# Attention and mixture of experts on one core: expert 0's rows transposed on TensorE, its list made tile by tile, and three steps moved

## The reference

```python
x = x + xattn(layernorm(x), ctx)      # 16 heads of 32; 2048 keys; q, k, v and the
                                      # probabilities rounded to 8-bit steps
n = layernorm(x)
w = golden_weights(n, Wr, temperature)   # a weight per token and expert, most are 0
x = x + sum_e w[:, e] * ((silu(n @ Wg[e]) * (n @ Wu[e])) @ Wd[e])   # 8 experts, F = 512
```

## Time and profile before

| | before |
|---|---|
| median of 3 runs | 807.9 us (807.88, 807.9, 809.99) |
| the profiled execution, its own time | 809.75 us |
| its span in the trace | 807.8 us |
| TensorE busy | 626.9 us (78%) |
| VectorE busy | 585.9 us (73%) |
| ScalarE busy | 449.8 us (56%) |
| GpSimd busy | 378.2 us (47%) |
| mean granted TensorE clock | 0.907 |

### The profile page before, as it was taken

How to read it: one execution, slowest core, us unless ns; L and a number is a source line. 1 busy time by engine, 2 the same in 40 slices (tenths; PEclk the granted TensorE clock), 3 DMA queues, 4 the chain that set the end, 5 groups by cost and what they waited for, 6 DMA issues and landing times.

```text
span 807.8 us, 15841 instructions
## 1 busy us (share of the span) xinstructions
PE 626.9 (78%) x4937; PEld 293.1 (36%) x4937; DVE 585.9 (73%) x1096; ACT 449.8 (56%) x519; POOL 378.2 (47%) x422
## 2 busy tenths in 40 slices
PE   2999898665867676777777654039999999999993
PEld 0444333132434242434333333014444444444441
DVE  4897687998999999999999954707446365374430
ACT  4243347587888888888888882004343443353321
POOL 2354343634566676767575751113353344334403
PEclk9999989698999998988999976559999999999997
DMA  8967749699998989898989895365987966967714
GB/s 246 263 139 163 167 79 165 120 175 210 173 167 167 186 168 183 163 188 156 196 155 201 153 191 134 97 195 83 232 217 164 243 170 172 254 140 204 140 15 54
DMA packets 339468, 134.97 MB, mean 167 GB/s; under 512 B 313700, under 2 KB 313700, under 8 KB 339432
## 3 DMA queue, kind: packets, MB, share of 16 engines
q1 hardware_dynamic: 332264, 117.76, 67.9%
q0 software_dynamic: 7168, 16.78, 10.2%
HBM read 44.33 MB, written 12.58 MB: 70 GB/s over the span
## 4 chain that ended last, share of the span: by engine, by line
PE 38%; issue 15%; SPq 14%; DMA 12%; DVE 9%; POOL 8%; ACT 2%; POOLq 1%; DVEq 0%; ACTq 0%
PE psum L1286 35%; DMA work<-work 8%; SPq L402 7%; SPq L313 2%; DVE spare L1082 2%; POOL work L563 2%; ACT work L820 1%; SPq L387 1%; POOL work L586 1%; PE psum L1393 1%; PE psum L1450 1%; DMA work<-x_rows,slot_tok 1%; DVE work L916 1%; DMA token_region<-work 1%; DMA work<-in_L_xattn_Wq_dram 1%
## 5 line engine op out<-in xcount | busy, mean ns | idle before, releaser
L820 ACT ACTIVATE work<-spare,exp_bias 128x2048 uint8<-128x2048 f32 (+1 forms) x128 | 256.2, 2002 | 54.3 <-DVE exp_bias L1089 47.2
L1082 DVE TENSOR_SCALAR_CACHE_REDUCE spare<-psum,q_step_now,s_first 128x1024 f32<-128x1024 f32 x128 | 171.0, 1338 | 1.5 <-PE psum L1393 1.3
L1082 DVE TENSOR_SCALAR_CACHE_REDUCE spare<-psum,q_step_now 128x1024 f32<-128x1024 f32 x128 | 164.4, 1286 | 5.9 <-PE psum L1393 5.8
L563 POOL CAST work<-work 128x2048 int16<-128x2048 uint8 x64 | 120.9, 1894 | 91.7 <-DMA work<-work 78.3
L1393 PE MATMUL psum<-keys_region,work 128*128 128x512 f16 x256 | 91.3, 456 | 42.8 <-DVE spare L1082 39.8
L667 POOL DMA_INDIRECT work<-x_rows,slot_tok x32 | 51.8, 1618 | 120.6 <-DVE slot_w L1226 81.2
L1359 PE MATMUL psum<-values_region,work 128*128 128x32 f16 x2048 | 73.0, 179 | 37.6 <-DMA work<-work 35.0
L1393 PE MATMUL psum<-keys_region,bias_hl 128*128 128x512 f16 x256 | 80.8, 413 | 27.3 <-DVE spare L1082 27.3
L1286 PE MATMUL psum<-work,spare 128*128 128x512 f16 x384 | 86.2, 385 | 18.4 <-DMA work<-work 18.4
L1359 PEld LDWEIGHTS psum<-values_region,work 128*128 128x128 f16 x2048 | 69.0, 98 | 84.3 <-DMA work<-work 54.0
L679 POOL DMA_INDIRECT out_dram<-keys_region,slot_tok x32 | 50.4, 1576 | 85.6 <-ACT keys_region L882 78.0
(11 more groups left out here) (188 smaller groups left out, 905.4 us busy)
## 6 DMA issues: line engine op xcount, KB each, us to landing
spare<-in_L_ffn_Wg_dram SPq DMA_DIRECT2D x8, 1024.0 KB
spare<-in_L_ffn_Wu_dram SPq DMA_DIRECT2D x8, 1024.0 KB
spare<-in_L_ffn_Wd_dram SPq DMA_DIRECT2D x8, 1024.0 KB, 14.2
work<-in_ctx_dram SPq DMA_DIRECT2D x4, 1024.0 KB, 6.2
work<-work SPq DMA_TRANSPOSE x192, 3.9
token_region<-in_L_xattn_Wkv_dram SPq DMA_DIRECT2D x2, 1024.0 KB, 8.3
resid<-in_x_dram SPq DMA_DIRECT2D x2, 1024.0 KB, 8.2
x_rows<-work SPq DMA_DIRECT2D x8, 256.0 KB, 2.2
```

Of the source, the lines that this page charges most:

```text
L563: nc.gpsimd.tensor_copy(p_T_int[h % 4 // 2], pair_bytes[h % 4 // 2]).then_inc(unpacked, 1)
L820: nc.scalar.activation(p_int[h % 4], scores, ACT.Exp, bias=exp_bias[:, h % 4:h % 4 + 1], scale=-1.0, accum_out=p_sum[:, h:h + 1]).then_inc ...
L1082: nc.vector.tensor_scalar(staged[h % 4][:, 1024 * c:1024 * c + 1024], psum[:, 2 * slot:2 * slot + 2, :].rearrange("p b k -> p (b k)"), q_s ...
```

## The change

- The Newton steps of tile 6 leave GpSimd; VectorE takes them, ahead of tile 7's last division, with its own helper `rsqrt`. GpSimd goes to `unpack(7, 14)` at once.
- The transposition of attention half 0 moves from behind head 13 to behind head 15, in all eight tiles.
- VectorE makes an identity of 128 columns (`ident`). All three weight cuts of expert 0 stand ahead of the gating: two before the addition of the projection, one behind tile 7's rows.
- `first_list`: TensorE multiplies expert 0's list tile by tile, behind each comparison, into four banks.
- SyncE no longer transposes expert 0's rows. It loads the gate weights of expert 1, waits for the four gathers, and loads the other two.
- `turn_rows`: TensorE multiplies each gathered tile with the identity, eight products of 128 columns; ScalarE and VectorE copy the high and the low half out of the banks. The first gate product is made in two halves of 256 columns: tiles 0 and 1 are turned, then the first half is multiplied, then tiles 2 and 3 are turned, then the second half is multiplied.
- The loops over the experts are laid out anew, with expert 0 ahead of the loop on TensorE.

```diff
@@ -172,6 +172,7 @@
...
+        ident = view(query_region, 2048, P // 2, F16)
...
...
+        ident_ready = sem("ident_ready")
+        rows_turned, rows_out = ([sem(f"{n}{l}") for l in range(2)] for n in ("rows_turned", "rows_out"))
...
@@ -405,7 +407,7 @@
                         load_weights(0, 0, [(h - 9) // 2])
                     if h == 4 and not first:
                         transpose_attention(i - 1, 1)
-                    if h == 13:
+                    if h == H - 1:
                         transpose_attention(i, 0)
                     if h == 7 and after_rows:
                         store_rows(i - 2)
@@ -431,8 +433,13 @@
                 i0 = k0 // 2
                 if k0:
                     load_weights(k0, 0)
-                load_weights(k0 + 1, 1)
-                transpose_selected(i0, 0)
+                    load_weights(k0 + 1, 1)
+                    transpose_selected(i0, 0)
+                else:
+                    load_weights(1, 1, [0])
+                    for landed in gathered[0]:
+                        sp.wait_ge(landed, 16)
+                    load_weights(1, 1, [1, 2])
                 with sp.Fori(0, E // 2 - 1) as i:
                     transpose_selected(i + i0, 1)
                     load_weights(2 * i + 2 + k0, 2 * i + 2)
@@ -653,8 +660,6 @@
             with pool.Fori(2, QT - 1) as i:
                 attention_tile(i, True, True)
             attention_tile(QT - 1, True, False)
-            deviation(QT - 2)
-            pool.sem_inc(deviation_ready, 1)
             unpack(QT - 1, 14)
 
 
@@ -887,6 +892,11 @@
                 if k0:
                     for m in range(3):
                         cut_weights(k0, 0, m)
+                else:
+                    for t in range(DK):
+                        act.wait_ge(rows_turned[0], t + 1)
+                        nc.scalar.activation(x_sel_T[0][:, t, 0:DK, :].rearrange("p k t -> p (k t)"), bank(4 + 2 * (t % 2)), ACT.Copy
+                                             ).then_inc(rows_out[0], 1)
                 with act.Fori(0, E // 2 - 1) as i:
                     expert(i + i0, 0, True)
                     expert(i + i0, 1, True)
@@ -1110,19 +1120,36 @@
             with dve.Fori(1, QT) as i:
                 attention_tile(i, False)
             make_bias(QT - 1, H - 1)
-            invert_sums(QT - 1, 1)
+
+            def rsqrt(own, var, y, t):
+
+                own.link(nc.vector.tensor_scalar(y.bitcast(I32), var.bitcast(I32), -0.5, float(RSQRT_GUESS), ALU.mult, ALU.add))
+                scale = 1.0
+                for _ in range(3):
+                    own.link(nc.vector.scalar_tensor_tensor(t, y, var, y, ALU.mult, ALU.mult))
+                    own.link(nc.vector.scalar_tensor_tensor(y, t, 3.0 * scale ** 2, y, ALU.subtract, ALU.mult))
+                    scale = -2.0 * scale ** 3
+                own.link(nc.vector.tensor_scalar(y, y, 1.0 / scale, None, ALU.mult))
 
             def rows_low(j):
                 dve.wait_ge(x1_hi, j + 1)
                 nc.vector.tensor_tensor(x1_hl[:, 1, :], x1_norm, x1_hl[:, 0, :], ALU.subtract).then_inc(x1_cut, 1)
 
-            dve.wait_ge(deviation_ready, 1)
-            nc.vector.tensor_scalar(x1_norm, x1, x1_mean[:, :], ln1_y[:, :], ALU.subtract, ALU.mult).then_inc(x1_normed, 1)
+            var, y, t = ln_a[:, 0:1], ln_rstd[:, 0:1], ln_b[:, 0:1]
+            dve.wait_ge(x1_squared, QT - 1)
+            own.link(nc.vector.tensor_scalar(var, x1_square[:, :], 1.0 / D, LN_EPS, ALU.mult, ALU.add))
+            rsqrt(own, var, y, t)
+            nc.vector.tensor_scalar(x1_norm, x1, x1_mean[:, :], y, ALU.subtract, ALU.mult).then_inc(x1_normed, 1)
+            dve.wait_ge(q_now_ready, 4 * QT)
+            own.link(nc.vector.tensor_copy(slot_now[:, :], token[:, 2, :]))
+            nc.vector.tensor_scalar(ident, slot_row[:, 0:P], slot_now[:, 0:1], None, ALU.is_equal).then_inc(ident_ready, 1)
+            invert_sums(QT - 1, 1)
             rows_low(QT - 2)
             divide(QT - 1, 1)
             dve.wait_ge(att_hi, 2 * QT)
             nc.vector.tensor_tensor(att_hl[:, 1, 1, :], att[:, 256:512], att_hl[:, 1, 0, :], ALU.subtract).then_inc(att_cut, 1)
             cut_weights(0, 0, 0)
+            cut_weights(0, 0, 1)
             dve.wait_ge(stored, 16 * (QT - 1))
             for half in range(2):
                 add_projection(QT - 1, half, bank(half)[:, 0:256])
@@ -1130,17 +1157,11 @@
             own.after(own.n)
             own.link(nc.vector.bn_aggr(ln1_mv[:, :], ln1_stats[:, :, :].rearrange("p n s -> p (n s)")))
 
...
+            rsqrt(own, var, y, t)
+            nc.vector.tensor_scalar(x1_norm, x1, ln1_mv[:, 0:1], y, ALU.subtract, ALU.mult).then_inc(x1_normed, 1)
             rows_low(QT - 1)
+            cut_weights(0, 0, 2)
 
 
             def tokens(v):
@@ -1207,20 +1228,21 @@
             own.link(nc.vector.copy_predicated(slot, mask.bitcast(I16), place))
 
 
-            def select_tokens(own, e, first_slot):
+            def select_tokens(own, e, first_slot, first=False):
 
                 own.link(nc.vector.tensor_scalar(slot_now[:, :], slot[:, :, bass.ds(e, 1)].rearrange("p t a -> p (t a)"),
                                                  float(-first_slot), None, ALU.add))
                 for t in range(QT):
                     ins = nc.vector.tensor_scalar(select[:, t, :], slot_row[:, :], slot_now[:, t:t + 1], None, ALU.is_equal)
-                ins.then_inc(select_ready, 1)
-
-            def slots(own, i, par):
+                    if first or t == QT - 1:
+                        ins.then_inc(select_ready, 1)
+
+            def slots(own, i, par, first=False):
 
                 k = 2 * i + par
                 dve.wait_ge(list_full, k + 1)
                 dve.wait_ge(y_added[DK - 1], 16 * before(k, 1))
-                parts = bank(7)[:, 0:5 * DK].rearrange("p (s c) -> p s c", c=5)
+                parts = psum[:, 4:4 + DK, 0:5] if first else bank(7)[:, 0:5 * DK].rearrange("p (s c) -> p s c", c=5)
                 own.link(nc.vector.tensor_reduce(slot_tok_f[:, :], parts[:, :, 0:2], AX.X, ALU.add))
                 own.mark(nc.vector.tensor_copy(slot_tok[par][:, :], slot_tok_f[:, :]))
                 nc.vector.tensor_reduce(slot_w[par][:, :], parts[:, :, 2:5], AX.X, ALU.add).then_inc(slots_ready, 1)
@@ -1258,10 +1280,16 @@
             def experts(k0, first_slot, base):
                 i0 = k0 // 2
                 own = Steps(dve, dve_step, base)
-                select_tokens(own, 0, first_slot)
-                slots(own, i0, 0)
-                for m in range(0 if k0 else 1, 3):
-                    cut_weights(k0, 0, m)
+                select_tokens(own, 0, first_slot, not k0)
+                slots(own, i0, 0, not k0)
+                if k0:
+                    for m in range(3):
+                        cut_weights(k0, 0, m)
+                else:
+                    for t in range(DK):
+                        dve.wait_ge(rows_turned[1], t + 1)
+                        nc.vector.tensor_copy(x_sel_T[0][:, t, DK:2 * DK, :].rearrange("p k t -> p (k t)"), bank(5 + 2 * (t % 2))
+                                              ).then_inc(rows_out[1], 1)
                 base = base + own.n
                 n = DK + 3
                 with dve.Fori(0, E // 2 - 1) as i:
@@ -1441,9 +1469,32 @@
             ins.then_inc(count_full, 1)
 
 
+            def first_list():
+
+                for t in range(QT):
+                    pe.wait_ge(select_ready, t + 1)
+                    for s in range(DK):
+                        ins = nc.tensor.matmul(bank(4 + s)[:, 0:5], select[:, t, s * P:s * P + P], tok_w[:, t, 0, :],
+                                               start=t == 0, stop=t == QT - 1)
+                ins.then_inc(list_full, 1)
+
+            def turn_rows(t):
+
+                pe.wait_ge(gathered[0][t], 16)
+                for l in range(2):
+                    pe.wait_ge(rows_out[l], max(t - 1, 0))
+                    for c in range(DK):
+                        ins = nc.tensor.matmul(bank(4 + 2 * (t % 2) + l)[:, c * P:c * P + P], x_sel[0][:, t, l * D + c * P:l * D + c * P + P],
+                                               ident, start=True, stop=True)
+                    ins.then_inc(rows_turned[l], 1)
+
+            def rows_taken(n):
+                for l in range(2):
+                    pe.wait_ge(rows_out[l], n)
+
             def list_slots(i, par, e):
                 k = 2 * i + par
-                pe.wait_ge(select_ready, k + 1)
+                pe.wait_ge(select_ready, k + QT)
                 pe.wait_ge(slots_ready, k)
                 for s in range(DK):
                     for t in range(QT):
@@ -1452,10 +1503,15 @@
                                                start=t == 0, stop=t == QT - 1)
                 ins.then_inc(list_full, 1)
 
-            def expert(i, par, e, following):
+            def expert(i, par, e, following, first=False):
                 k = 2 * i + par
```

(31 more changed lines are left out.)

10 lines of the change are left out of this document (removed).

## The result

The changed kernel takes 795.3 us (median of 4 runs, 794.26 to 796.2). The profiled execution took 796.2 us for a span of 794.1, 13.7 less than the span of before.

The account below looks back on a forecast made before the run. TensorE paces the experts and waits elsewhere; time removed ahead of its start at 537.89 was to count in full. Median 807.9 − 7.5 (+0.9 and −0.8 contained, attention loop nothing) = 800.4; range 798.4 to 804.2.

Parts of the forecast that it names:

- The attention loop: Attention loop: SyncE's 15.3 us wait at head 13 goes, but VectorE paces the loop; taken as nothing, bounds −2 and +1.
- Rival 4: End of attention costs +3 instead of +0.9 (802.5), or the loop gains 2 (798.4); chance 0.08, a third to the low side.
- The end of attention: Last tile: project(7) waits for the moved transposition, with the products of heads 15 and 14 behind it; +0.9, bounds 0 and +3.
- The list tile by tile: Expert 0's first list: 28 of 32 products run under the comparisons, 4 are left; −0.8, bounds −0.9 and 0.
- The Newton steps, the identity and the third cut: VectorE's added work at the end of attention and before the gating: fits in its idle time, costs nothing.
- The seam: Slots ready to the list of expert 1: quicker gathers and rows turned on TensorE instead of by DMA; −7.6.
- Rival 1: Expert 0's start: TensorE's pause keeps the clock low, second half product takes 2.6 instead of 1.3; +1.8, 802.2; chance 0.18.
- Rival 2: Turning expert 0's rows: each product waits for its 128-column load, at double price; 802.8 to 804.4; chance 0.09.
- Rival 3: Expert 0's gathers don't land sooner, the last at 532, second half product moves by 2.4; 802.8; chance 0.08.
- Rival 5: Tile seams of the loop: moved transposition stands ahead of the next heads 0 and 1, 7 × 1.5 us; 810.9; chance 0.04.

Follow-up runs that it names:

- the one line alone: Kernel before with only half 0's attention transposition moved from behind head 13 to behind head 15: 803.1 us, ratio 0.994.

## Why the prediction was wrong, and where it was right

**The step that failed** is "The attention loop. SyncE waited 15.3 us in six places for GpSimd's cut at head 13; that wait goes. But VectorE paces the loop and idled only 7.1 us for TensorE in 330 us: bounds −2 and +1, taken as nothing." It measured −4.9 in the changed kernel and −4.5 with the one line alone (tiles 2 to 7: −5.2 and −5.1), about as much as the 5.1 us by which the forecast missed; the other differences, from +1.9 at the seam to −1.5 ahead of the loop, nearly cancel. Two things in it were wrong. The place of the wait was assumed: the six waits are behind head 4 of the next tile, 19 us further on, and the times of the six issues would have shown it. What costs is the place of half 0's transposition ahead of head 14, which makes GpSimd late with the cut of half 1, holds the queue and makes the heads behind it late. And the bound of −2 was worked out from no row: of the 7.1 us of VectorE's idle time 3.9 lay in tiles 2 to 7, and all of that went. A tile's length, read from its first score to the next one's, gives more still: tiles 3 to 6 took 0.65 to 1.1 us more than tile 2 of the same trace (40.72), 3.6 together. With tile 7 taken like them, the bound on the low side should have been about −4.5. Rival 4's "the loop gains 2" had the sign and not the size.

**The end of attention** was forecast at +0.9 and came out at −0.5. The order of waits was right (project(7) stands for half 0, the heads behind it), and the size was off: half 0 was to land 7.2 us behind the last exponential and landed 5.1 behind it. The queue was taken as late. In the earlier trace rows head 15's transposition came 3.1 us after its exponential, the forecast took 1.5 off, and it came 0.3 us after. With half 0 still ahead of head 14 and only the hold in the loop gone (half 1 at head 5) it came 1.0 us after, so most of this is the same miss again.

**The list tile by tile**: −0.7 for −0.8. **The Newton steps, the identity and the third cut**: nothing, as forecast; the gating's first step is 8.13 us behind the statistics, before 8.15.

**The seam**: −5.7 for −7.6, and −7.8 where the clock was early. Its terms held one by one: first gather 1.24 (forecast 1.55), the others 0.95; landing 3.3 to 3.8 (3.9 or more; the forecast's 525.9 for the first landing is 0.8 above its own start plus 3.9, which changes nothing, as tile 1's landing decides); eight turning products 1.01 (0.86 and a drain of 0.17); half products 2.72. TensorE's pause ahead of a half product is 0.88 us, for some 0.8 forecast. That the loads had to be held by SyncE's wait was not so. **Rival 1, the late clock**, is what the profiled execution of the changed kernel did, and its price of 1.8 measured 2.0. It happened in three of seven traces, so that 0.18 was too small a chance. It did not show in the total: without the loop's 4.9 the saving would have been 7.7 for the 7.5 forecast, and that this comes so near is in part luck, as the seam gave 1.9 less, the end of attention 1.4 more, and the trace is 1.5 shorter ahead of the loop.

**Rival 2** did not happen. A turning product costs 0.13 us at the low level of the clock and under 0.08 at the high one. The rule of the Trainium skill, "TensorE: Matmul & The Clock Gate", part 4, on transposing products (275 ns each) would have made an estimated 8.8 us of the 32. The Trainium skill gives this price for a transpose mode of the instruction, not for plain products. The trace has 1.01, 1.03 and 1.91 for these plain ones, together 3.95. **Rival 3** did not happen either. **Rival 5**, that the moved transposition would hold the queue at every seam, had the mechanism, a transposition in the wrong place that holds a full queue, and the wrong place: it was the old place that did this, some 5 us in all. The moved one costs no tile anything (40.63).

## What to carry to other kernels

In a loop that one queue serves nearly without slack, ask of every wait of that queue at which issue it stands and what is behind it, and read the loop's period, not the busy engine's idle time. The period shows what the idle time hid: a tile took 40.63 us where it had taken 41.4 to 41.8. An entry in the queue costs by what it makes late: here 1.6 us ahead of one head came back 19 us later as a wait for another engine, and moving the entry by one head was worth 5.2 us in the loop, where the rewrite of the seam was worth 5.7. A stage that starts with the clock low and waits for data first can be given work that nobody reads, if it ends before the data lands.
